# Cross-attention and a quantised FFN on one core: x of batch 2 loaded among the first rows, w2 after the rows of batch 1

## What is computed

```
x   = x + attention(layernorm(x), ctx)          # 32 query heads, 8 key/value heads of 16, masks
x   = x + ffn(layernorm(x))
ffn(x) = bitlinear(layernorm(gelu(silu(bitlinear(x, w1, b1)))), w2, b2)
bitlinear(x, w, b): x -> rms norm, rounded to 8 bits per token;
                    w -> round(w / mean|w|) in {-1, 0, 1}, times mean|w|
```

## Time and profile before

| | us |
|---|---|
| median of 3 runs | 617.34 (617.25 to 619.74) |
| the profiled execution | 618.85 |
| its span, first to last instruction | 616.8 |

### The profile page before, as it was taken

One profiled execution on the slowest core, in us unless ns is written; L12 is line 12 of the kernel. 1 busy time (PEld: TensorE's weight loads), 2 busy tenths in 40 slices (PEclk: granted clock), 3 DMA queues, 4 the chain that ended last, 5 costly groups with the idle time before them and its releaser, 6 DMA issues.

```text
span 616.8 us, 8915 instructions
## 1 busy us (share of the span) xinstructions
PE 516.5 (84%) x3374; PEld 284.2 (46%) x3374; DVE 490.3 (79%) x728; ACT 351.9 (57%) x424; POOL 137.9 (22%) x105
## 2 busy tenths in 40 slices
PE   4927496598989999999999999999959987797656
PEld 4816322364346455645564456445514542333332
DVE  4519972779489988898889889988996899828895
ACT  2204186214865877487648764786468548578721
POOL 5102031110341052105210431131121102403030
PEclk9976889679998999999999999999969997989888
DMA  6797269625621661257125711472126211200000
GB/s 214 238 296 284 92 195 330 186 78 197 145 56 41 200 162 38 75 186 176 37 74 166 192 42 41 162 189 49 40 60 142 62 41 36 53 1 0 35 35 35
DMA packets 32995, 72.17 MB, mean 117 GB/s; under 512 B 7168, under 2 KB 14530, under 8 KB 29951
## 3 DMA queue, kind: packets, MB, share of 16 engines
q1 hardware_dynamic: 31222, 67.06, 37.1%
q0 software_dynamic: 576, 4.19, 2.1%
q10 hardware_dynamic: 1152, 0.31, 0.3%
HBM read 46.50 MB, written 20.61 MB: 109 GB/s over the span
## 4 chain that ended last, share of the span: by engine, by line
PE 56%; DVE 15%; DMA 9%; ACT 8%; issue 7%; POOL 1%; SPq 1%; ACTq 0%; DVEq 0%
PE FF L862 8%; PE PV L802 7%; PE FF L680 6%; PE PV L785 6%; PE FF L911 6%; ACT PT L1083 6%; PE S L769 5%; PE S L743 5%; DVE negm L1356 5%; PE PV L743 2%; DMA denc<-x 2%; PE FF L864 2%; DMA num<-o_raw 2%; DMA x_sb<-in_x 2%; PE FF L876 2%
## 5 line engine op out<-in xcount | busy, mean ns | idle before, releaser
L1083 ACT ACTIVATE PT<-S 128x1024 f32<-128x1024 f32 x128 | 123.6, 1031 | 29.1 <-PE S L769 28.7
L1356 DVE TENSOR_REDUCE negm<-S 128x4 f32<-128x1024 f32 x88 | 105.6, 1214 | 20.8 <-PE S L743 19.1
L769 PE MATMUL S<-Q,K 100*128 100x512 bf16 x256 | 76.3, 404 | 25.4 <-ACT PT L1083 17.4
L743 PE MATMUL S<-K,Q 97*128 97x256 bf16 x352 | 54.8, 282 | 28.3 <-DVE rest L1329 12.9
L862 PE MATMUL FF<-w1t,xqT 128*128 128x512 bf16 x256 | 67.1, 385 | 8.0 <-ACT work L1114 4.3
L785 PE MATMUL PV<-PT,vaug 128*32 128x256 f32 x1024 | 71.9, 401 | 0.6 <-ACT PT L1083 0.6
L802 PE MATMUL PV<-wo_sb,num 128*128 128x512 f32 x128 | 60.9, 621 | 0.7 <-DVE negm L1356 0.6
L1114 ACT ACTIVATE work<-FF,s 128x512 f32<-128x512 f32 x56 | 38.4, 687 | 40.4 <-PE FF L864 40.3
L743 PEld LDWEIGHTS S<-K,Q 97*128 97x128 bf16 x352 | 34.0, 100 | 51.1 <-issue 17.4
L1356 DVE TENSOR_REDUCE negm<-PV 128x4 f32<-128x1024 f32 x40 | 48.8, 1220 | 6.0 <-PE PV L743 5.6
L769 PEld LDWEIGHTS S<-Q,K 100*128 100x128 bf16 x256 | 18.1, 99 | 74.5 <-ACT PT L1083 54.6
(11 more groups left out here) (197 smaller groups left out, 855.9 us busy)
## 6 DMA issues: line engine op xcount, KB each, us to landing
Q<-q_d SPq DMA_DIRECT2D x15, 768.0 KB
q_d<-part SPq DMA_DIRECT2D x8, 768.0 KB, 3.6
x_sb<-in_x SPq DMA_DIRECT2D x8, 512.0 KB, 3.5
ctx_sb<-in_ctxT SPq DMA_DIRECT2D x8, 512.0 KB, 4.0
work<-in_w SPq DMA_DIRECT2D x4, 1024.0 KB, 13.5
q_d<-part SPq DMA_DIRECT2D x8, 512.0 KB, 3.2
xb_sb<-in_x SPq DMA_DIRECT2D x8, 512.0 KB, 4.2
work<-in_w POOLq DMA_DIRECT2D x4, 1024.0 KB, 15.6
```

What stands on the lines that cost most here:

```text
L743: last = pe.matmul(to[:, r, :], Q[0:ROWS_1, g, r, t * P:(t + 1) * P], K[0:ROWS_1, g, :], start=not masked, stop=True)
L769: last = pe.matmul(where, K[0:ROWS_2, g, kt * P:(kt + 1) * P], Q[0:ROWS_2, g, 2 * pair:2 * pair + 2, :], start=not masked, stop=True)
L1083: act.activation(PT[:, n % PT_SLOTS, :, :], ST[n % 2][:], ACT.Exp, scale=0.25).then_inc(S["pt_made"], 1)
L1356: dve.tensor_reduce(negm[:, t, R * g:R * g + R], RING_1[n % 3][:], AX.X, ALU.max, negate=True).then_inc(S["max_made"], 1)
```

## The change

Two transfers get another place, with the steps that depend on them. x of batch 2 is issued between the second and the last group of batch 0's rows, and no longer after them. VectorE takes its statistics behind the second maximum of batch 0; before, it did so ahead of query_rests(1). key_rests(1) now stands ahead of the first maximum. TensorE transposes x of batch 2 after score 7 instead of score 2, and its four projections stand after the scores 8, 10, 12 and 14 instead of 5, 8, 11 and 14. ACT sums chunk 0 of w1 ahead of the copy of x of batch 2. w2 waits on GpSimd for the second half of batch 1's rows as well as for w1_done, and stands behind norm_1(3) and its application. The reciprocal of batch 0's denominators moves from behind maximum 2 to behind maximum 4.

```diff
@@ rows_back_first (SP)
                 for gs, landed in ((slice(0, 2), "rows_first"), (slice(2, 4), "rows_in0"), (slice(4, 8), "rows_in1")):
+                    if landed == "rows_in1":
+                        load_x(2)
                     sp.dma_start(Q[0:ROWS_SPLIT, gs, :, :].rearrange("d g r t -> d (g r t)"),
@@ body of SP
                     rows_back_first()
-                    load_x(2)
                     for n in range(1, 4):
                         weight_chunk(w1, n)
@@ second_weights (GpSimd)
                 pool.wait_ge(S["w1_done"], 1)
+                pool.wait_ge(S["rows_in1"], 16 * ROW_LOADS * 2)
                 for n in range(4):
@@ body of GpSimd
-                if at_start(c):
-                    second_weights()
                 if w is not None and w + 1 < B:
                     norm_1(w + 1)
                     norm_1_apply(w + 1)
+                if at_start(c):
+                    second_weights()
@@ batches (TensorE)
                     scores_1(0, n, masked)
-                    if n == 2:
+                    if n == 7:
                         turn_x(2)
-                    if n in (5, 8, 11, 14):
-                        project_q(2, [(n - 5) // 3])
+                    if n in (8, 10, 12, 14):
+                        project_q(2, [(n - 8) // 2])
@@ body of ACT
+                    weight_abs_sum(0, range(1))
                     turned_x(2)
-                    weight_abs_sum(0)
+                    weight_abs_sum(0, range(1, 4))
@@ body of VectorE
                     key_masks()
-                    norm_1(2)
                     query_rests(1)
-                    maximum(0, 0)
                     key_rests(1)
-                    for n in range(1, 16):
+                    for n in range(16):
                         maximum(0, n)
+                        if n == 1:
+                            norm_1(2)
@@ body of VectorE, the loop over the maxima
-                    if c is not None and n == 2:
+                    if c is not None and n == (4 if at_start(c) else 2):
                         reciprocal(c)
```

## The result

| | before | after |
|---|---|---|
| median, us | 617.50 (4 runs, 617.25 to 619.74) | 610.75 (4 runs, 609.40 to 611.15) |
| profiled execution, us | 618.85 | 610.75 |
| its span, us | 616.8 | 608.7 |

The account below looks back on a forecast made before the run. Bound by two transfer waits in the first 150 us: x of batch 2 and batch 0's last denominators. Gains of 7.9 (first scores) and 8.0 (batch 1's maxima) sum to 15.9, from 617.34 to 601.4 us; range 596.5 to 608.

Parts of the forecast that it names:

- I take 37.0, behind the first packet: First stage, TensorE: score 0 starts at 37.0 us, after the first 16 KB instruction-queue packet (36.6 to 36.8); bounds 34.5 and 43.2.
- The second packet: First stage: if score 0 also needs the instruction packet at 42.8 to 43.2, everything is 6.2 us later, gain 1.7.
- The rule of the Trainium skill: Branch before score 0: a target outside the fetched window must be fetched first; score 0 not before 36.8, without it 34.5.
- From there TensorE sets the pace: First stage from 50.3 us: four projections and seven scores take 10.0 us, against 9.2 for eight maxima; stage ends at 62.0.
- The first projection still at half clock: Bound for the first stage: it ends at 63.8 us instead of 62.0, gain 6.1 instead of 7.9.
- x, VectorE, GpSimd, and the hidden costs: First stage: x lands near 39.1, no VectorE wait, turn_x(2) at 47.3; moved loads, w1 sums and SP's chain stay covered.
- The wait for the denominators: Second stage: VectorE's 9.46 us wait before the reciprocal goes; the last denominators land at 102.5, cover about 1 us.
- (a) The division ... I take 118.1, 1.5 late: Second stage: batch 0's quotient, due at 116.6 for project_out, comes at 118.1 because w2 slows the reciprocal rows.
- The bound of 124: Second stage: quotient at some 124 us if hindered by w2 as the denominators were; unhindered 112.9.
- the signs of being wrong: New profile: score 0 at 43 or later, VectorE or GpSimd idle over 3 us, TensorE idle before weight_sum, or gain lost later.
- (b) The sum of w2 ... 121.5, 0.9 late: Second stage: w2's last chunk, due at 120.6 for weight_sum, lands at 121.5; 115 alone, 128 with other transfers before it.
- Rival 2: Half the gain given back: page at 43 needed or w2 late by 3.5 to 5; 603.5 to 608, both up to 612; 0.23.

Follow-up runs that it names:

- the first part alone: Changed kernel with only the first-stage edits (x of batch 2, batch 0's maxima), w2 and the reciprocal as before the change: 614.48 us, ratio 0.9964.
- the reciprocal at 3: Changed kernel with the reciprocal of batch 0's denominators behind maximum 3 instead of 4: 612.16 us, ratio 0.9911.
- the early branch: Changed kernel with TensorE's mask-flag branch moved ahead of the second half of batch 1's query projection: 614.58 us, ratio 0.9937; two further runs combine it with other edits.

## Why the prediction was wrong, point by point

- **What bounds the kernel now** was read rightly: both waits were removed by the change and nothing behind batch 1 moved.
- **TensorE, "I take 37.0, behind the first packet".** The mechanism was right, the size was not, and this is the first of the two terms that failed. The forecast let score 0 run 0.4 us after the packet began to move; it came 3.0 us after that in the changed kernel, 3.1 in the first part alone and with the reciprocal at 3. Part of this stood in the earlier trace rows: 32.7% of 16 engines over 0.2 us are 1.05 us on one engine, so the packet did not end at 36.8 but near 37.7, later than the 37.0 that was taken. And the packet itself began at 38.6, 1.9 us later than in the earlier trace rows, of which 1.1 are the start. Score 0 was 3.5 us later than forecast, the start taken off. The second packet (45.8 us) was not needed: score 0 was before it.
- **The rule of the Trainium skill** (Runtime: NRT & Kernel Launch, Instruction fetch mechanics), by which a taken branch has to fetch its page first: the runs without a branch agree with it, with 6.1 us at the end of the stage. The stall was 4.4 to 4.8 us with the DMA engines nearly idle and 6.0 to 8.4 with them full.
- **"From there TensorE sets the pace"** was right: from the first projection to the start of the last score it took 11.2 us (54.81 to 66.02), where 10.0 were said. "The first projection still at half clock" was one of the bounds (1.8 us more) and is what happened: 3.56. Projection and copy began 3.4 us later than said, the start taken off, as score 0 did.
- **x, VectorE, GpSimd, and the hidden costs** held: no wait for x, 6.8 us from norm_1's begin to turn_x(2) (44.91 to 51.74; forecast 7.3), score 8 not held by its rows, w1's sums and SP's chain in time.
- **The wait for the denominators** went whole: 9.95 us with all around it, forecast 9.46. The rows of batch 1 had landed at 99.94, 3.8 us after the issue of the last denominators (96.14), where 4.4 had been estimated.
- **"(a) The division ... I take 118.1, 1.5 late"** is the second term that failed. It was 4.5 us late. The chain from the issue of the store to the quotient took 16.1 us, where the forecast had 13.7 (104.4 to 118.1) and the kernel before 8.5. The forecast laid all that w2 costs, 5.2 us, on the load of the reciprocal rows and left the store in front of it as it was, at 1.5 us. It was the store that w2 held up: 7.5 us, 6.0 more. The load took 6.3 instead of 4.7, 1.6 more, because by then w2 was nearly through and SP's queue had 44.5% of the engines, close to the 40% that the forecast had taken. Where the store was ahead of w2 (reciprocal at 3), the load ran in w2's full flight, with 14.6%, and took 13.6: the 13.5% of the earlier trace rows, and the upper end of the estimate. The rest of the 3.0 us, about 0.6, is that TensorE was ready sooner than said (114.0, against 116.6 less the 1.9 gained up to there). The bound of 124 (in its terms 7.4 late) held it, and of the signs of being wrong this one came true: GpSimd idle on the reciprocal rows by more than 3 us (13.10).
- **"(b) The sum of w2 ... 121.5, 0.9 late"**: it was in time. w2 landed 13.1 us after its first issue, near the 12 it needs alone, because the small transfers beside it gave way and the layer rows were issued only at 112.67, when it was nearly in. By the Trainium skill (DMA: Bandwidth & Descriptors, Queues, rings and completion order) the engines go round the queues by packet, and w2 would have come at 124 and cost 3.5 us; in the frame of the forecast it came at about 115.6. That both queues have their turn, no run here contradicts, but an even share in bytes does not follow from it: in 103 to 115 with the reciprocal at 3, both had work, and it was 3.92 MB to 0.54.
- **Rival 2**, half given back, names the size but not the causes: the page at 43 was not needed, and w2 was not late. Its end with both losses was 612 and had been left out of the range. The two misses, 5.8 us at the end of the first stage (3.5 fetch, 1.1 start, 1.2 clock and rounding) and 3.0 at the quotient, less 0.5 at the denominators and less 0.3 for a quicker project_out (5.84 against 6.11), are the 8.0 us between the forecast and the 7.9 of the traces. The profiled executions differ by 8.1 and the medians by 6.75, since that of the kernel before stood 1.35 us above its median.

## What to carry to other kernels

An idle stretch in front of an instruction can hide a fetch as well as a wait: when the wait is removed, look for a branch behind the last instruction and for the small packets of the instruction queue, and count on from the packet to the first instruction (3.0 us here). A large transfer on one queue does not only share with the small ones of another, it can starve them (7.5 us for 32 KB here, 1.5 without it). If a chain goes through DRAM beside it, price every step of the chain, the smallest too. In the marks it paid, by 3.7 us, to hold the large transfer until the store was through and to move what was not due (the layer rows) out of the stage; in the medians this is not clear of the scatter. And read the granted clock before an idle is blamed for it: in front of project_out it was at 0.50 four microseconds ahead of the idle.

## What was not expected of the hardware

- From the start of the packet of the instruction queue to the first matmul behind the branch: 3.0 to 3.3 us in seven traces with full DMA engines, 2.6, 2.6 and 3.0 in the three with the early branch, where the engines were nearly idle.
- The split of the DMA engines between w2 on GpSimd's queue and small transfers on SP's: 98.0 to 1.9% over 8 us with a store of 32 KB outstanding, which took 7.5 us and takes 1.5 with the engines nearly idle, and 86.9 to 14.6% over 12 us with 0.5 MB of loads.
- GpSimd's issue of w2 at 100.56 had little in flight before 102: the DMA share was 0.19 at 100 to 102.
- A cast and a subtraction of 128 x 64 on VectorE that take 0.20 and 0.22 us took 2.22 and 2.30 (at 116.24 and 118.50 us of the changed kernel) while GpSimd multiplied and added 128 x 1024. Nothing waited for them here. Why they took so long was not tried.
